# Axial attention with MLP and Mamba: scores by single head with keys unpadded, a third value buffer, and W1 in float32r parts

## The reference, cut to what matters

```
# layer 0: E = 256, H = 8 heads, d_k = 32, N = 64
q, k, v1, v2 = x @ Wq, x @ Wk, x @ Wv1, x @ Wv2           # (B, N, N, H, d_k)
scores = einsum('bilhd,bljhd->biljh', q, k) / sqrt(d_k)
att = softmax(scores, axis=2)                             # over l
out = einsum('biljh,bilhd,bljhd->bijhd', att, v1, v2)
h = layer_norm(x + out.reshape(B, N, N, E) @ Wo)
h = layer_norm(relu(h @ W1 + b1) @ W2 + b2 + h)
# layer 1: four Mamba2 passes over rows and columns, joined by a linear layer
```

## Time and profile before

| | us |
|---|---|
| median of three runs | 2490.59 |
| profiled execution | 2494.16 |
| span of the profiled execution | 2492.3 |
| PE busy | 2126.9 (85%) |
| DVE busy | 2015.0 (81%) |
| ACT busy | 1287.2 (52%) |
| POOL busy | 1014.1 (41%) |

### The profile page before, as it was taken

One profiled execution on the slowest core, in us unless ns is written; L12 is line 12 of the kernel. 1 busy time (PEld: TensorE's weight loads), 2 busy tenths in 40 slices (PEclk: granted clock), 3 DMA queues, 4 the chain that ended last, 5 costly groups with the idle time before them and its releaser, 6 DMA issues. The chain is left out here.

```text
span 2492.3 us, 42420 instructions
## 1 busy us (share of the span) xinstructions
PE 2126.9 (85%) x16632; PEld 1389.7 (56%) x16632; DVE 2015.0 (81%) x2393; ACT 1287.2 (52%) x2690; POOL 1014.1 (41%) x513
## 2 busy tenths in 40 slices
PE   8999866776677766665999978999999999999998
PEld 7877411231132211113777756777777777777776
DVE  4426699979988999994777767888888888888886
ACT  3337567657756764541232334555555555555553
POOL 1103699979988999991110001111112111111111
PEclk9999999989999999998999998999999999999999
DMA  7668322124121212103332215232222323333332
GB/s 236 232 211 249 90 61 36 28 52 85 20 51 28 36 19 40 25 12 86 95 96 78 87 39 111 69 73 71 69 75 72 80 77 89 93 94 92 85 77 60
DMA packets 302502, 204.43 MB, mean 82 GB/s; under 512 B 202720, under 2 KB 280032, under 8 KB 297696
## 3 DMA queue, kind: packets, MB, share of 16 engines
q1 hardware_dynamic: 293600, 168.17, 27.8%
q0 software_dynamic: 8704, 33.56, 3.7%
HBM read 133.76 MB, written 67.90 MB: 81 GB/s over the span
## 5 line engine op out<-in xcount | busy, mean ns | idle before, releaser
L330 DVE TENSOR_TENSOR att_av<-att_att,att_v2ps 128x2816 f32<-128x2816 f32 (+2 forms) x288 | 775.4, 2751 | 53.6 <-PE att_bank L509 52.5
L330 POOL TENSOR_TENSOR att_av<-att_att,att_v2sb 128x1280 f32<-128x1280 f32 x256 | 745.2, 2931 | 79.7 <-PE att_bank L509 75.1
L509 PE MATMUL att_bank<-att_av,att_w 128*32 128x512 f32 x4096 | 532.9, 624 | 252.0 <-DVE att_av L330 219.6
L509 PEld LDWEIGHTS att_bank<-att_av,att_w 128*32 128x32 f32 x4096 | 131.2, 111 | 592.7 <-issue 333.3
L650 ACT ACTIVATE att_ev<-att_bank 128x512 f32<-128x512 f32 x512 | 299.0, 596 | 300.1 <-PE att_bank L509 229.9
L1693 DVE SCALAR_TENSOR_TENSOR mb_cv<-mb_bank,mb_cw,mb_cv 128x504 f32<-128x504 f32 (+2 forms) x480 | 343.1, 730 | 126.4 <-ACT mb_cv L1516 121.3
L1336 POOL TENSOR_TENSOR mb_rstd<-mb_ms,mb_neghalf 128x4 f32<-128x4 f32 x32 | 32.3, 1009 | 793.6 <-DVE mb_ms L1737 793.6
L1397 PE MATMUL mb_bank<-mb_xT_hi,dt_win_hi 128*128 128x512 f32 x576 | 241.7, 420 | 36.8 <-DVE mb_cv L1693 35.4
L1455 PE MATMUL mb_bank<-mb_wf,mb_y 128*128 128x256 f32 x1024 | 245.1, 387 | 0.6 <-DVE mb_y L1733 0.6
L1397 PE MATMUL mb_bank<-mb_xT_lo,dt_win_hi 128*128 128x512 f32 x576 | 229.0, 398 | 0.0
L1397 PE MATMUL mb_bank<-mb_xT_hi,dt_win_lo 128*128 128x512 f32 x576 | 228.7, 397 | 0.0
(11 more groups left out here) (182 smaller groups left out, 3326.1 us busy)
## 6 DMA issues: line engine op xcount, KB each, us to landing
att_xin<-in_x SPq DMA_DIRECT2D x32, 512.0 KB, 4.4
qk_t<-att_qk POOLq DMA_DIRECT2D x16, 1024.0 KB, 5.1
v<-att_vs POOLq DMA_DIRECT2D x16, 1024.0 KB, 5.2
mixed_t<-att_ev SPq DMA_DIRECT2D x1024, 8.0 KB
mb_dAb<-dA_rows SPq DMA_DIRECT2D x32, 512.0 KB, 5.7
mb_dAb<-dA_cols SPq DMA_DIRECT2D x32, 512.0 KB, 6.1
att_q<-qk_t SPq DMA_DIRECT2D x8, 1024.0 KB, 9.8
att_kb<-qk_t SPq DMA_DIRECT2D x128, 64.0 KB, 2.1
```

The lines of the kernel that those rows point to most:

```text
L330: return eng.tensor_tensor(av[t % 2][:, :, d0:d1, :], a.unsqueeze(2).broadcast_to((P, 2, d1 - d0, N)), v2.unsqueeze(1).broadcast_to((P, 2, ...
L509: mm = pe.matmul(bank[r % NB][s * M:(s + 1) * M, :], w[i // WB % 2][:, i % WB, s, :], av[r // 2 % 2][:, i % 2, s * STRIP_D:(s + 1) * STRIP ...
```

## The change

It has three parts.

1. **Scores.** Group g now covers head g % 2 of the pair and eight l: 2 batches x 8 l = 16 matmuls with 32 contraction rows and 64 columns, where there were 8 with 64 rows and 128 columns. `kb` holds keys as they lie in DRAM, [128, 16 l, 64 j], in four chunks of 16 l. Each chunk comes in two transfers of 256 KB, where a chunk of 8 l came in four of 64 KB. The zeroing of `kb` and SP's wait for it are gone. In the pair loop, key chunks 2 and 3 stand behind the stores e = 0 and e = 1.
2. **Values.** `vs` has three buffers (`NV`).
3. **MLP's W1.** POOL splits W1 once into hi and lo; ACT's copy of h's transpose gives the hi part, DVE subtracts to give the lo part (`low_of_hT`, between its two adds at line 1075), and PE makes three float32r products per k in place of one float32 product. `times_wo` and `mlp` wait for the lo part.

```diff
@@ block_attention
+    L8 = 8
-    KL = 8
+    KL = 16
-    NX = 4
+    NX, NV = 4, 3
-        kb = [sb(f"kb{u}", [P, 2, KL, N]) for u in range(2)]
+        kb = [sb(f"kb{u}", [P, KL, N]) for u in range(2)]
-            vs = [e_.sb(f"vs{u}", [P, TT, 2 * E]) for u in range(2)]
+            vs = [e_.sb(f"vs{u}", [P, TT, 2 * E]) for u in range(NV)]
@@ load_k(n, c)
-                    for h2 in range(2):
-                        lo = (2 * b + h2) * DK
-                        src = qk_dram[E + n * 64 + h2 * DK:E + n * 64 + (h2 + 1) * DK,
-                                      b * N * N + c * KL * N:b * N * N + (c + 1) * KL * N]
-                        sp.dma_start(kb[c % 2][lo:lo + DK, h2, :, :], src.rearrange("p (l j) -> p l j", l=KL))\
-                            .then_inc(k_loaded[c % 2], 16)
+                    src = qk_dram[E + n * 64:E + (n + 1) * 64, b * N * N + c * KL * N:b * N * N + (c + 1) * KL * N]
+                    sp.dma_start(kb[c % 2][b * 64:(b + 1) * 64, :, :], src.rearrange("p (l j) -> p l j", l=KL))\
+                        .then_inc(k_loaded[c % 2], 16)
@@ SP, pair loop
-                    if c % 2 == 0 and n < PAIRS:
-                        for k in {0: (2, 3), 1: (4, 5), 2: (6,), 3: (7,)}.get(e, ()):
-                            load_k(n, k)
+                    if c % 2 == 0 and n < PAIRS and e in (1, 2):
+                        load_k(n, e + 1)
                     store(c, e)
@@ gpsimd
-            for u in range(2):
-                pool.memset(kb[u][:, :, :, :], 0.0).then_inc(kb_zeroed, 1)
@@ scores(n, g)
-                for l4 in range(LB):
+                for i in range(L8):
+                    l = g // 2 * L8 + i
                     for b in range(B):
-                        r = slice(b * 64, (b + 1) * 64)
-                        mm = pe.matmul(X_[g % 2][r, l4 * P:(l4 + 1) * P], qv[r, g * LB + l4, :],
-                                       kb[c % 2][r, :, (g * LB + l4) % KL, :], start=True, stop=True)
+                        r = slice((2 * b + g % 2) * DK, (2 * b + g % 2 + 1) * DK)
+                        mm = pe.matmul(X_[g % 2][b * 64:(b + 1) * 64, i * N:(i + 1) * N], qv[r, l, :],
+                                       kb[c % 2][r, l % KL, :], start=True, stop=True)
@@ copy_scores(n, g)
-                act.activation(raw[:, :, :, g * LB:(g + 1) * LB],
-                               X_[g % 2][:, :].rearrange("p (l h j) -> p j h l", l=LB, h=2), ACT.Copy, scale=-SCALE)\
+                act.activation(raw[:, :, g % 2, g // 2 * L8:(g // 2 + 1) * L8],
+                               X_[g % 2][:, :].rearrange("p (l j) -> p j l", l=L8), ACT.Copy, scale=-SCALE)\
@@ evict_v, on ACT and on DVE
-                    need(dve, v_stored[v % 2], v // 2 * 16)
+                    need(dve, v_stored[v % NV], v // NV * 16)
@@ block_mlp
+            pool.wait_ge(w_loaded, 32)
+            for k in range(KT):
+                pool.tensor_copy(w1_["hi"][:, k], w1[:, k]).then_inc(w1_split, 1)
+            pool.wait_ge(w1_split, KT)
+            for k in range(KT):
+                pool.tensor_tensor(w1_["lo"][:, k], w1[:, k], w1_["hi"][:, k], ALU.subtract).then_inc(w1_split, 1)
@@ times_wo and mlp
-                need(pe, hT_ready, 2 * c)
+                need(pe, hT_lo_ready, 2 * c)
-                    for k in range(KT):
-                        mm = pe.matmul(HID_[m][:, :], w1[:, k, m * P:(m + 1) * P], hT[u][:, k, :],
-                                       start=(k == 0), stop=(k == KT - 1))
+                    for n, (k, xn, wn) in enumerate([(k, xn, wn) for k in range(KT) for xn, wn in SPLIT]):
+                        mm = pe.matmul(HID_[m][:, :], w1_[wn][:, k, m * P:(m + 1) * P], hT[xn][u][:, k, :],
+                                       start=(n == 0), stop=(n == 3 * KT - 1))
@@ DVE
+            def low_of_hT(c, u):
+                if c < NCHUNK:
+                    for k in range(KT):
+                        dve.wait_ge(hT_hi_ready, 2 * c + k + 1)
+                        dve.tensor_tensor(hT["lo"][u][:, k, :], WO_[k][:, :], hT["hi"][u][:, k, :], ALU.subtract)\
+                            .then_inc(hT_lo_ready, 1)
@@ back(c, u)
                                       hb[u][:, s, :], ALU.add).then_inc(w2_added, 1)
+                    if half == 0:
+                        low_of_hT(c + 1, 1 - u)
```

More of the change, by code:

```diff
@@ L169, in block_attention @@
         w = [sb(f"w{u}", [P, WB, STRIPS, M]) for u in range(2)]
-        ident_set, kb_zeroed, q_loaded = sem("ident_set"), sem("kb_zeroed"), sem("q_loaded")
+        ident_set, q_loaded = sem("ident_set"), sem("q_loaded")
         k_loaded = [sem(f"k_loaded{u}") for u in range(2)]
@@ L181, in block_attention @@
         qk_by, v_by = [[sem(f"{n}_by_{e}") for e in ("act", "dve")] for n in ("qk", "v")]
-        qk_stored, v_stored = [[sem(f"{n}_stored{u}") for u in range(2)] for n in ("qk", "v")]
+        qk_stored = [sem(f"qk_stored{u}") for u in range(2)]
+        v_stored = [sem(f"v_stored{u}") for u in range(NV)]
         v2_in_sb, v2_in_ps, v2_read = sem("v2_in_sb"), sem("v2_in_ps"), sem("v2_read")
@@ L220, in block_attention, with values_stored @@
         block = ctx.enter_context(nc.Block())
+        def values_stored(eng, chunks):
+            for u in range(NV):
+                eng.wait_ge(v_stored[u], len(range(u, chunks, NV)) * 16)
         @block.sync
@@ L270, in _ @@
                 load_x(u)
-            sp.wait_ge(kb_zeroed, 2)
             for u in range(2):
@@ L279, in _ @@
             load_k(0, 2)
-            load_x(XN + 7)
+            for v in (7, 8):
+                load_x(XN + v)
             load_k(0, 3)
[L282 to L288, removed]
+            for v in (9, 10):
+                load_x(XN + v)
             load_q(1)
@@ L293, in _ @@
                 load_x(XN + v)
-            for u in range(2):
-                sp.wait_ge(v_stored[u], XN // 4 * 16)
+            values_stored(sp, XN // 2)
             load_v2(0)
@@ L299, in _ @@
             load_x(XN + 15)
-            for u in range(2):
-                sp.wait_ge(v_stored[u], XN // 2 * 16)
+            values_stored(sp, XN)
             for c in range(NC):
@@ L362, in _ @@
                     pool.wait_ge(v_by[e], 2 * v + 2)
-                pool.dma_start(v_out[v], vs[v % 2][:, :, :]).then_inc(v_stored[v % 2], 16)
+                pool.dma_start(v_out[v], vs[v % NV][:, :, :]).then_inc(v_stored[v % NV], 16)
             for t in range(PAIRS * STEPS):
@@ L474, in scores @@
                 if g * LB % KL == 0:
-                    pe.wait_ge(k_loaded[c % 2], (n * (N // KL // 2) + c // 2) * 64 + 64)
+                    pe.wait_ge(k_loaded[c % 2], (n * (N // KL // 2) + c // 2) * 32 + 32)
                 if g < 2 and n == 0:
@@ L612, in copy_att @@
                 if n == 1 and g == 0:
-                    for u in range(2):
-                        act.wait_ge(v_stored[u], XN // 2 * 16)
+                    values_stored(act, XN)
                 act.activation(att[n % 2][:, :, g * JB:(g + 1) * JB],
@@ L673, in evict_v @@
                 if tile == 0:
-                    need(act, v_stored[v % 2], v // 2 * 16)
+                    need(act, v_stored[v % NV], v // NV * 16)
                 act.wait_ge(v_done, TT * v + tile + 1)
-                act.activation(vs[v % 2][:, tile, :], bank[(TT * v + tile) % NB][:, :], ACT.Copy).then_inc(v_by[0], 1)
+                act.activation(vs[v % NV][:, tile, :], bank[(TT * v + tile) % NB][:, :], ACT.Copy).then_inc(v_by[0], 1)
             xT_hi(0)
@@ L761, in block_mlp @@
         hb = [sb(f"hb{u}", [P, TT, E]) for u in range(2)]
-        hT = [sb(f"hT{u}", [P, KT, CHUNK]) for u in range(2)]
+        hT = {n: [sb(f"hT{u}_{n}", [P, KT, CHUNK], F32R) for u in range(2)] for n in ("hi", "lo")}
+        w1_ = {n: sb(f"w1_{n}", [P, KT, F], F32R) for n in ("hi", "lo")}
         hid = sb("hid", [P, FT, CHUNK])
@@ L778, in block_mlp @@
         f_chain, b_chain = sem("f_chain"), sem("b_chain")
-        h_ready, h_turned, hT_ready = sem("h_ready"), sem("h_turned"), sem("hT_ready")
+        h_ready, h_turned, hT_hi_ready, hT_lo_ready = sem("h_ready"), sem("h_turned"), sem("hT_hi_ready"), sem("hT_lo_ready")
+        w1_split = sem("w1_split")
         hid_done, hid_ready, w2_done, w2_added = sem("hid_done"), sem("hid_ready"), sem("w2_done"), sem("w2_added")
@@ L910, in mlp @@
             def mlp(c, u):
-                pe.wait_ge(hT_ready, 2 * c + 2)
+                pe.wait_ge(hT_lo_ready, 2 * c + 2)
                 for i, m in enumerate(ORDER):
@@ L940, in _ @@
             pe.wait_ge(w_loaded, 32)
+            pe.wait_ge(w1_split, 2 * KT)
             for c in range(NCHUNK):
@@ L962, in copy_hT @@
                     act.wait_ge(h_turned, 2 * c + k + 1)
-                    act.activation(hT[u][:, k, :], WO_[k][:, :], ACT.Copy).then_inc(hT_ready, 1)
+                    act.activation(hT["hi"][u][:, k, :], WO_[k][:, :], ACT.Copy).then_inc(hT_hi_ready, 1)
             def copy_x1T(c):
@@ L1119, in _ @@
             front(0, 0)
```

(1 more changed line is left out.)

2 lines of the change are left out of this document (1 added, 1 removed).

## The result

The changed kernel takes 2512.64 us (median of six runs, 2502.35 to 2515.81) beside 2494.11 for the kernel before in the same runs. The ratio is 1.0066, 95% interval 1.0051 to 1.0080: 0.7% slower. The forecast was 2494 beside 2490.59, no change; the same ratio on 2490.59 is 2507, above the forecast's own range of 2482 to 2504 and inside the wide one of 2470 to 2511. The profiled execution's span is 2513.1 us, 20.7 above that of before, and that difference can be placed.

What follows compares the result with a forecast made beforehand. PE was taken to bound MLP (DVE near) and values, with SP-queue waits in the loops. +11.0 + 1 + 8.7 - 17.5 = +3.2 on the profiled 2494.16 gave 2497.4, less 3.6: 2494 us; own range 2482 to 2504, 80% range 2470 to 2511.

Steps and rivals of the forecast that it cites:

- second rival: MLP: DVE becomes the loop's bound, the period stays at 19.87 us and the MLP gives 0; 2511 us, chance 0.08.
- A group of scores, +0.88 us: Attention scores: the strided weight load sets the pace, about 113 ns a pair, 1.81 us a group, +0.88 us each.
- The loops, +11.0: Pair loops: dearer groups give 154.6 us against 143.6 over three loops, SP's waits gone but for 1.7; +11.0 us.
- The next pair's loads near step 25, +1: Pair loops: half a megabyte more in flight for the next pair's first chunks and q; +1 us, bounds 0 and +4.
- Values, +8.7: Value stage: sixteen groups +14.1, third buffer -6.2, first score's wait for a larger key chunk +0.8; +8.7 us together.
- -6.2: Value stage: third buffer removes ACT's store wait, -4.82 for PE and -1.4 for the half-clock stretch after it.
- MLP, -17.5: MLP: float32r W1 shortens the period from 19.87 to 18.67 us; -17.5 us, bounds 0 and -22.4.
- the load not bound by its stride: Attention scores: a group costs 0.94 us and loop groups cost nothing; 2453 us, chance 0.13.
- DVE as the bound of the MLP: MLP: DVE's chain, 18.3 us, passes 19.9 and the gain is lost; 2511 us, chance 0.08.
- first rival: Scores' load not bound by stride: value stage -4.8 (0.6 + 0.8 - 6.2), loops -16; 2453 us, chance 0.13.
- SP's waits: Pair loops: rival that larger key chunks load too slowly, so all 31.2 us of waits return; 2525 us, chance 0.06.

Runs made afterwards that it cites:

- one_a_step: Changed kernel with one group of scores in each of the first sixteen steps, where one and two took turns in the first eleven; 2498.68 us, ratio 1.0015.
- q_unit: Changed kernel with q read at unit stride too, operands of the score matmuls exchanged (keys as weights); output not the reference's; 2459.76 us, ratio 0.9861.
- old_kl16: Kernel before, block-diagonal keys kept, with key chunks of 16 l in four 128 KB transfers and the changed kernel's order of SP's queue; 2470.85 us, ratio 0.9899.
- scores_alone: Kernel before with only the scores part (single heads, keys as they lie, new SP order), two value buffers, float32 W1; 2528.91 us, ratio 1.0129.

## Why the prediction was near and where it failed

The terms of the sum were 17.5 us too low together, more than five times the change that they forecast, and the result lies outside the range made from them. It lies inside the wide range, whose upper end was set for a second rival that did not come true in that way; that much is luck.

- **A group of scores, +0.88 us.** Right in kind and nearly in size: +0.83 beside a step with one group and beside the values (3.30 / 4), +0.67 for each of two (5.17 - 3.84 = 1.33). A pair takes 111 ns by the starts of its records, forecast 113. The second of two groups is cheaper because its first few pairs, which are of the other head's rows, run between the last pairs of the first group: around 511.9 pairs start 50 to 60 ns apart. No run alternates the heads all along. The reason given was half of it. I let the weight load alone set the pace; with unit-stride weights the moving q keeps the same pace, and only both at unit stride free it.
- **The loops, +11.0.** The waits for SP went as forecast, and with them the lower clock that stood behind them, which the prediction had counted as waiting. And eleven undisturbed steps would be 6 x 3.78 + 5 x 5.17 = 48.5 us, 7.5 less than forecast over three loops. The step that failed is the granted clock: every term of the loops stood at full clock. Steps of 5.1 to 5.5 us with one group cost 4.7, 5.4 and 5.9 us in the three loops, 16 together, worked out as the excess over 3.78. With 0.6 more at the first loop's start that makes the 163.8 where I had 154.6. In the trace of before the slow stretches stood behind waits, and I took idle time for their cause; here PE is busy when the clock falls, and `one_a_step` and `q_unit` showed that it stays up when the stretches of scores are shorter.
- **The next pair's loads near step 25, +1.** It was +5.3 (8.98 and 9.54 us where 6.72 and 6.50 stood), over my upper bound of 4. The bytes grew there and the issues did not: `old_kl16`, with as many bytes in the eight issues of before, has 8.4 and 9.5. That fits a wait on the DMA engines, and cutting the loads into pieces moved it.
- **Values, +8.7.** +5.9 by the stage. From one chunk's first matmul to the next, the four chunks with scores are 2.7, 3.3, 3.3 and 3.3 us longer, 12.6 in all, where the groups and the wait for a larger key chunk had 14.9. The two chunks that stalled are 6.7 shorter, for the -6.2 forecast. That the -6.2 may be added to the groups is not shown: beside the new scores the stall was already down to half (`scores_alone`).
- **MLP, -17.5.** The period of 18.67 came out at 18.70. The sum failed in three other places, 10.4 us together. One is the first chunk (4.7), whose period was 4.2 us longer where I had a net -0.5: POOL's splitting of W1, costed at 0, took 2.3 of DVE's time while PE waited; DVE's layer norm came 1.2 later, as the first product with Wo took 6.67 us for 5.10, at a clock of 0.55 for 0.72; and the -1.2 was not to be had, since no product with W1 stands in this period. The others are the second and third, where before already had 19.66 and 18.70 so that -1.2 each was not to be had either (2.3); and the last twelve, 4.1 more, since the periods in which DVE goes round slower than PE cost 4.9 us where I had allowed 1.2, and the plain gain was 1.16 and not 1.2. Against that the last chunk gave 0.7 more. The doubt about DVE was right; POOL's part, put at 0.3 us, is 1.4 in each of two periods, and dt's small work on DVE was left out.
- The rivals: the load not bound by its stride is out, its 2453 being nearly what the kernel takes once there is no stride. DVE as the bound of the MLP came true in four periods, the two of 20.2 us beside POOL and those of 19.5 and 19.4. In the first rival's sum, sixteen groups at 0.94 us for 0.93 are +0.2 and not +0.6. SP's waits did not stay.

The errors of +9.2 and +4.3 in the loops, +10.4 in the MLP and -2.8 in the values, with -2.7 for the later steps of the loops and -0.9 for the rest, add to 17.5: that is by how much the span's +20.7 passed the forecast's +3.2.

## What to carry to other kernels

Before halving a matmul to save multiplications by zero, look at how its operands are read: a strided read that lies hidden beside a matmul of 128 columns is the pace of one of 64, on the stationary and on the moving side alike. Price rearranged TensorE work at both clock levels, since the level can fall while PE is busy. And when a part of a change costs, try its by-products apart: here the order of one DMA queue was worth 25 us, and the matmuls that came with it cost more.

## What was not expected of the hardware

- A long busy stretch of strided 32x64 score records (3.38 us, 64 of them) was followed by rows at a granted clock of 0.57, with no idle PE before, in 11 of 15 cases; the same records in stretches of 1.99 us left it at 1.00 over 60 us.
- A stride of 256 bytes costs a moving operand of 64 float32 columns as much as a stationary one: two groups in 3.34 and 3.38 us, and 1.84 with neither.
- POOL's cast and subtraction from SBUF to SBUF hold up DVE's TENSOR_SCALAR beside them: four take 3.69 or 2.76 us for 1.38. The Trainium skill, GPSIMD Engine Reference, section "1. Specifications", says that GpSimd shares its SBUF interfaces with VectorE and contends with those of its instructions that run in a 2-port mode or have two inputs in SBUF. The rows agree that there is contention and give the price; in which mode these four ran no trace shows.
